# Two transfers between rests on GpSimd in the last third of a mixture-of-experts and attention kernel, and the first row's scatters one visit sooner

## The reference: what is computed

```python
x = x + 0.5 * ffn(layernorm(x), W1, b1, W2, b2, Wg, bg)      # 4 experts, each token takes one
x = x + attention(layernorm(x), Wq, Wk, Wv, proj)            # linear attention with elu + 1 features
x = x + 0.5 * ffn(layernorm(x), W1, b1, W2, b2, Wg, bg)
# ffn: idx = argmax(softmax(x @ Wg + bg)); y = gelu(x @ W1[idx] + b1[idx]) @ W2[idx] + b2[idx]
```

## Time and profile before

| | us |
|---|---|
| median of three runs | 273.23 |
| lowest and highest | 270.52, 274.24 |
| the profiled execution | 272.48 |
| its span, first to last instruction | 270.8 |
| GpSimd busy | 171.6 (63% of the span) |
| TensorE matmul busy | 211.7 (78%) |
| VectorE busy | 165.8 (61%) |
| mean granted TensorE clock | 0.948 of full speed |

### The profile page before, as it was taken

How to read it: one execution, slowest core, us unless ns; L and a number is a source line. 1 busy time by engine, 2 the same in 40 slices (tenths; PEclk the granted TensorE clock), 3 DMA queues, 4 the chain that set the end, 5 groups by cost and what they waited for, 6 DMA issues and landing times. The chain is left out here.

```text
span 270.8 us, 6178 instructions
## 1 busy us (share of the span) xinstructions
PE 211.7 (78%) x1676; PEld 198.7 (73%) x1676; DVE 165.8 (61%) x670; ACT 123.6 (46%) x377; POOL 171.6 (63%) x234
## 2 busy tenths in 40 slices
PE   4978679959996998868689798987686897729920
PEld 3967569959996996758579797866675896729920
DVE  2768834588766566998886746998853442222310
ACT  2221356625568593324436966334354365215600
POOL 4405888820688870230277881488588888888886
PEclk9999799979998999999999999999999799798995
DMA  5994698751193440336029442248147463423011
GB/s 132 347 276 130 234 290 289 208 190 58 48 329 107 141 143 1 135 146 238 4 61 338 140 134 70 92 166 305 52 146 269 142 212 108 139 90 140 29 40 39
DMA packets 28448, 41.67 MB, mean 154 GB/s; under 512 B 7792, under 2 KB 14848, under 8 KB 28416
## 3 DMA queue, kind: packets, MB, share of 16 engines
q1 hardware_dynamic: 24448, 34.24, 36.1%
q0 software_dynamic: 3072, 6.82, 9.1%
q10 hardware_dynamic: 896, 0.23, 0.4%
HBM read 9.40 MB, written 6.82 MB: 60 GB/s over the span
## 5 line engine op out<-in xcount | busy, mean ns | idle before, releaser
L1044 ACT ACTIVATE hT<-U,slab 128x128 f32<-128x128 f32 x304 | 86.6, 368 | 69.8 <-PE U L881 63.2
L881 PE MATMUL U<-hT_in,slab 128*128 (+1 forms) x608 | 86.7, 289 | 0.7 <-ACT hT_in L1038 0.7
L889 PE MATMUL DN<-W,hT 128*128 (+1 forms) x608 | 85.2, 286 | 0.0
L881 PEld LDWEIGHTS U<-hT_in,slab 128*128 128x128 f32 x608 | 79.1, 203 | 2.0 <-issue 1.2
L889 PEld LDWEIGHTS DN<-W,hT 128*128 128x128 f32 x608 | 77.4, 200 | 0.7 <-issue 0.2
L379 POOL DMA_INDIRECT G<-rows,src x64 | 62.5, 976 | 20.4 <-DVE src L617 11.0
L369 POOL MEMSET rest<- 128x512 f32 x95 | 49.8, 524 | 17.7 <-DVE G L655 8.3
L631 DVE TENSOR_SCALAR xn<-G 128x128 f32<-128x128 f32 x64 | 24.8, 397 | 32.0 <-DMA G<-rows,src 31.4
L655 DVE SCALAR_TENSOR_TENSOR G<-DN,mask,G 128x128 f32 (+1 forms) x76 | 26.5, 348 | 27.7 <-PE DN L889 21.7
L388 POOL DMA_INDIRECT out_dram<-G x32 | 32.2, 1006 | 5.6 <-issue 4.8
L872 PE MATMUL TR<-ident,xn 128*128 128x128 f32 x64 | 14.9, 308 | 26.6 <-DVE xn L631 24.5
(11 more groups left out here) (142 smaller groups left out, 207.4 us busy)
## 6 DMA issues: line engine op xcount, KB each, us to landing
slab<-W SPq DMA_DIRECT2D x76, 322.0 KB
rows<-G SPq DMA_DIRECT2D x8, 288.0 KB, 2.1
rows<-X SPq DMA_DIRECT2D x4, 512.0 KB, 7.4
X<-in_L_attn_x_dram SPq DMA_DIRECT2D x4, 256.0 KB, 6.3
W<-in_L_ffn_W_dram SPq DMA_DIRECT2D x1, 1024.0 KB, 9.5
X<-in_L_attn_x_dram SPq DMA_DIRECT2D x2, 512.0 KB, 7.3
W<-in_L_ffn_W_dram SPq DMA_DIRECT2D x4, 256.0 KB, 4.7
G<-rows,src POOLq DMA_INDIRECT x64, 2.6
```

The costliest lines, as they stand in the source:

```text
L881: i = eng.matmul(U[s % 3][:, c * P:(c + 1) * P], slab[s % NSLAB][:, c * P:(c + 1) * P], hT_in[ph % 2][:, bass.ds(v * P - expert_at[s], P)] ...
L889: i = eng.matmul(DN[s % 2][:, 0:D], hT[s % NHT][:, c * P:(c + 1) * P], W2[:, bass.ds(expert_at[s] + c * NE * D, D)], start=(c == 0), stop= ...
L1044: i = eng.activation(hT[s % NHT][:, c * P:(c + 1) * P], U[s % 3][:, c * P:(c + 1) * P], ACT.Gelu, bias=slab[s % NSLAB][:, F + c:F + c + 1])
```

## The change

The helper functions `gather` and `scatter` get a flag `second`. With it neither the wait for the transfer before nor the filling of `rest` is written, only the count goes on. It is set for:

- the second gather of a visit in row 1's second block (in phase 2, visits 13, 15 and 17);
- the scatter behind the gather in visits 12, 14, 16 and 18 of phase 2;
- the scatter behind the gather in visits 0 to 5 of phase 3.

That is 3 + 4 + 6 = 13 transfers. Row 0's scatters begin at visit 4 of phase 2 instead of 5, and without the `midway` wait, so that eight of them stand ahead of visit 12 instead of seven. All later scatters move up by one place. In phase 3 the scatters of visits 6 and 7 lose their `midway`.

```diff
-            def gather(f, b, t):
-                rested()
+            def gather(f, b, t, second=False):
+                if second:
+                    next(count)
+                else:
+                    rested()
...
-            def scatter(b, t):
-                rested()
+            def scatter(b, t, second=False):
+                if second:
+                    next(count)
+                else:
+                    rested()
...
-                    gather(f, b, 3 * k // 2 + 1)
+                    gather(f, b, 3 * k // 2 + 1, second=(f == 1 and b == 1))
...
-            HELD = FIRST1 - 5 + (V - FIRST1 + 1) // 2
+            HELD = FIRST1 - 4 + (V - FIRST1 + 1) // 2
...
-                if 5 <= v < FIRST1:
-                    midway(s)
-                    scatter(0, v - 5)
+                if 4 <= v < FIRST1:
+                    scatter(0, v - 4)
                 if v >= FIRST1 and (v - FIRST1) % 2 == 0:
                     midway(s)
-                    scatter(0, FIRST1 - 5 + (v - FIRST1) // 2)
+                    scatter(0, FIRST1 - 4 + (v - FIRST1) // 2, second=True)
...
                 if v + NEXT1 < T:
                     gather(1, 1, v + NEXT1)
-                if v + HELD < T:
                     midway(s)
-                    scatter(0, v + HELD)
-                elif v < 7:
-                    midway(s)
-                    scatter(1, v - 5)
-                elif v == 7:
-                    scatter(1, 2)
-                    midway(s)
-                    scatter(1, 3)
+                    if v + HELD < T:
+                        scatter(0, v + HELD, second=True)
+                    else:
+                        scatter(1, v - 4, second=True)
                 else:
                     scatter(1, v - 4)
```

## The result

The changed kernel takes **263.93 us** (median of 4 runs, 263.43 to 266.01), the one before 273.43 (the three runs of the table above and one more, 270.52 to 274.24). The ratio is 0.971, with a 95% interval of 0.965 to 0.977: faster, by 9.5 us. The profiled execution took 263.43 us, with a span of 261.4. In all that follows a ratio leaves out the executions more than 1.5% above the fastest of their kernel, and a median takes all.

A forecast was written before the change was run, and what follows sets the result against it. GpSimd's queue was taken as the bound: 60.8 instead of 71.7 us saves 10.9, less 0.9 at the start, 10.0; 272.48 - 10.0 = 262.5, and with the median 0.75 above the profiled execution, 263.0 predicted, range 259 to 274.

The forecast's parts named there:

- GpSimd's own queue bounds the end: From the gather at 196.41 on, only GpSimd's queue sets the time: 40 intervals of 1.79 us, 71.68 in all.
- The start, +0.9 us: Before the last stretch, visit 4's scatter delays the second power and routing; first gather at 197.3 instead of 196.41.
- 26 intervals at 1.79: Behind the last routing, 26 intervals still hold a rest and keep 1.79 us each, 46.5 us together.
- The removed `midway` waits: At the scatters that lose `midway`, removing the wait was held to be worth nothing.
- Thirteen at d = 1.1: Within the thirteen pairs, the second transfer starts 1.1 us after the first; together 14.3 us.
- the cases that I called stretched: Second transfers in the pairs are somewhat stretched, d from 1.2 to 1.44, time 264.2 to 267 us; chance 0.05.
- A power right behind a transfer shows that GpSimd is free: A power starts 0.97 us after a transfer's start, so the transfer has left GpSimd's cores by then.
- that rival: In the pairs, GpSimd needs some 1.8 us between transfers anyway; saving only 0.8 us, 271.7 us; chance 0.14.
- A second transfer waits for the first to land, 0.17: In each pair the second transfer ends about 2.59 us later than alone, d = 2.6, 282.1 us; chance 0.17.
- VectorE stretches second transfers: VectorE's port use could stretch all thirteen second transfers to d 1.5, saving 4.7 us, 267.8 us; not adopted.
- Cover at the end, 6.3 us: The last visit's result is there at 251.8, 6.3 us before the last scatter's place at 258.1.

The follow-up runs named there:

- The pairs alone: Kernel before with the thirteen second transfers lacking wait and rest, first scatter left at visit 5: 266.44 us, ratio 0.975.
- The experiment with the scatter at visit 8: Changed kernel with the extra scatter at visit 8, behind the four powers, instead of at visit 4: 265.17 us, ratio 0.968 to before.
- Pairs at the end: Changed kernel with the fourteen last scatters in seven pairs too: 263.21 us, ratio 0.961 to before.
- the kernel without rests: Changed kernel without rests or waits for the transfer before from visit 12 of phase 2 on: 255.16 us, ratio 0.932 to before.
- the one with its scatter moved: Changed kernel without rests or waits from visit 12 of phase 2 on, extra scatter at visit 8: 264.29 us, ratio 0.967 to before.
- early scatter only: Kernel before with only the scatter at visit 4 added early; every transfer keeps wait and rest: 271.07 us, ratio 0.990.
- the change again: Changed kernel unaltered, run once more on the second chip: 268.41 us, ratio 0.975 to before.
- the kernel with short rests: Changed kernel with every rest at 64 columns instead of 512, all its waits kept: 264.95 us, ratio 0.975 to before.

## Why the prediction was right

Faster was forecast with 0.69, 263.0 us, 259 to 274; it is 263.93. The range reaches up to the time of before, so it is the narrower range of the forecast itself, 259 to 266, that says something. The 0.75 us between the profiled execution and the median are in the forecast and in none of the rivals' times; that changes none of the cases. Point by point:

- *GpSimd's own queue bounds the end:* shown. The pairs alone shorten the queue by 6.8 us and the time follows (2.5%), and without any pace the queue ends 10.8 us sooner than with pairs (62.81 - 51.97).
- *The start, +0.9 us:* measured +0.67 (25.16 instead of 24.49). The second power is 0.89 late against the first one (0.95 forecast), the fourth 0.79, the `lgm` wait 1.01 (1.2 forecast). The experiment with the scatter at visit 8 shows the cause. The first gather's own time, 195.94 instead of 197.3, is earlier by 1.1 for the lead of this execution.
- *26 intervals at 1.79:* 1.78. A rest behind a pair does not grow. The removed `midway` waits, counted as nothing, were worth 0.12 at one place: the interval up to visit 5's scatter is 1.77, where it was 1.89 before with `midway` in it (177.21 to 179.10).
- *Thirteen at d = 1.1:* this is the term that was mis-sized. It is **1.27**: the transfer lasts 0.97 as before, but 0.30 lies between the two. I took the nearer end from a power that follows a transfer at once; a transfer behind a transfer needs more than an arithmetic instruction there. This costs 2.3 us of the forecast's 10.0 (thirteen times 0.174). With the start and the intervals, 0.2 and 0.3 better, that gives the 8.2. The lead of this execution, 1.1, made up for most of the missing 1.8 in the profiled time, and the medians are 9.5 apart, 1.3 more than the change accounts for. That 263.93 lies within 1 us of 263.0 is partly luck. By its number, 1.27 falls among the cases that I called stretched and gave 0.05; by its kind it does not, since second transfers take 0.94 to 1.05 and first ones 0.95 to 1.05.
- *A power right behind a transfer shows that GpSimd is free:* held, and it told against the rival with d = 1.8. But that rival was half right: with the wait kept and the memset gone, a second transfer does come only after 1.77. The prediction priced neither the wait nor the memset by itself; the change won because it dropped both.
- *A second transfer waits for the first to land, 0.17:* it did not come. On the first chip 40 in a row keep 1.27 in the median, while a gather lands 2.5 to 4.3 us after it starts. By the Trainium skill (Perfetto Trace Analysis, "DMA Instruction — SWDGE (GPSIMD)") more descriptors can be generated than fit in their buffer; no issue grew here with 40 transfers in a row, so no run here shows a full one. That the landings come later with pairs, up to 3.5 instead of 2.6, the prediction had allowed for under its cover.
- *VectorE stretches second transfers:* not here. The one long scatter of the routing is still there, 1.41 us in the kernel after, and no transfer of the pairs is like it. The Trainium skill (SBUF — State Buffer, "SBUF: two separate sides") has the two engines lock each other out for a whole instruction, and VectorE only in some of its instructions. The trace agrees for the norm beside a memset, 0.69 against 0.355. The transfers of the pairs show no such lock: they take 0.94 to 1.05 with VectorE active.
- *Cover at the end, 6.3 us:* 5.4. Gather to result took 20.7 instead of 19.75; the last gather's distance to the last scatter is the 26.1 of the forecast. "Pairs at the end" used 3.5 us of it without any wait.

**What stays open.** Why VectorE, ScalarE and GpSimd in some executions go on several us after TensorE's recorded end. The traces show where: on the second and third chip in the kernels with transfers 1.3 us apart, and not in the two there that keep 1.68 or more between them. With one trace for each, that is a pattern and not a cause. They do not show why the first chip is free of it, or whether it is the chip or the execution; the kernel without rests and the one with its scatter moved were not run on the same chip, and of the change there are two measurements with one trace each. That the rests were put in against this is my guess. What varies ahead of the change is another matter. The first power of phase 2 comes between 170.08 and 175.34 us in the kernels that keep their rests up to there. From 100 to 170 us the mean granted clock is 1.00 in before and after, 0.95 in "early scatter only" and the change again, where it fell to the lower of its two levels (1.2 of 2.4 GHz) for a few us, first at 120. What TensorE did just before does not tell them apart: from 116 to 120 it was busy for 1.84 of 4 us in "early scatter only", and for 2.54 in before, where the clock stayed. Nor is the clock all: the kernel with short rests has 1.00 in this stretch and its first power at 173.57. How much of the spread it makes stays open.

## What to carry to other kernels

Price the wait and the work behind it apart, and together: here either alone kept nearly all of what the two cost, so an experiment that takes away only one finds nothing, and only leaving out both gains. A pace that looks like waste may hold off a cost that appears in some executions only, so run such a change on more than one chip before its gain is believed: nearly the same kernel gave 255.2 us on one and 264.3 on another. And a gain at the tail of a queue is worth its full size only while the other engines' cover lasts: here TensorE's 0.89 per block took over from 241 us on.

## What the runs showed of the hardware

- An indirect transfer of this size occupies GpSimd for 0.97 us. The next one starts 1.24 to 1.30 after it if nothing is between (up to 1.37 behind a longer transfer), 1.66 to 1.69 with a memset of 0.52 between. Behind a wait for its issue it starts after 1.71 to 1.90 where another wait stands beside that one, whether a memset of 0.52, one of 0.15 or none lies between; where the wait for the issue stands alone, after 1.69 with a memset of 0.52 and 1.31 with one of 0.15.
- A gather of 128 rows of 144 numbers lands 2.6 us after its start at one transfer every 1.79 us, and 2.5 to 4.3 us after it at one every 1.27.
- The first gather starts 0.28 us after `src` is written if GpSimd's last instruction before was a memset (195.66 to 195.94 in the kernel after), and 0.78 after it in the kernel without rests (197.88 to 198.66; the profile names a later result of VectorE as what ended that wait).
- VectorE, ScalarE and GpSimd can stand still at once, VectorE for up to 6.9 us, and go on 4.9 us after TensorE's last recorded matmul, with no instruction in the records that would explain it.
